# Edge stages of a two-layer graph network: when x is copied, how far gathers run ahead, when zeros are written, and in which order GpSimd waits

## What is computed

```python
h = maximum(layernorm(x), 0)                                   # layer 0
msgs = (h @ W0.T)[dst] * edge_weight[:, None]
x = x + segment_sum(msgs, src, N)
h = maximum(layernorm(x), 0)                                   # layer 1
h2 = segment_sum(h[src], dst, N) + h
h1 = h2 @ W1 + b1                                              # 256 -> 1024
h1 = relu((h1 - mean(h1, 0)) * rsqrt(var(h1, 0) + 1e-5) * gamma + beta)
out = x + relu(h1 @ W2 + b2)
```

## Time and profile before

| | |
|---|---|
| median of three runs | 4040.16 us |
| the profiled execution, whole | 4048.41 us |
| its span on the core | 4045.5 us |
| granted TensorE clock, mean of the span | 0.937 |
| layer 0, until its first scatter | 0 to 173.5 us |
| layer 0, scatters of groups 0 to 48 | 173.5 to 793 us |
| layer 1, until its first scatter | 793 to 843.3 us |
| layer 1, scatters of groups 0 to 48 | 843.3 to 1455 us |
| Gram, normalisation, main stage | 1455 to 4045 us |

### The profile page before, as it was taken

The page is one execution under the profiler, slowest core; times in us unless marked ns, Lnnn a source line. Parts: engine busy times, 40 slices in busy tenths (PEclk is TensorE's granted clock), DMA queues, the critical chain, the costliest instruction groups (busy, mean ns, idle before and its releaser), DMA issues.

```text
span 4045.5 us, 58701 instructions
## 1 busy us (share of the span) xinstructions
PE 3550.6 (88%) x17911; PEld 3028.4 (75%) x17911; DVE 2161.8 (53%) x5128; ACT 2164.8 (54%) x3631; POOL 1039.7 (26%) x801
## 2 busy tenths in 40 slices
PE   0387787488777869999999999999999999999999
PEld 0277777476666757778888888888888888888888
DVE  0355555366655568845555455455554555554554
ACT  0244454332222269956666656666666566566665
POOL 6377777678878720000000000000000000000000
PEclk9888878788888889999999999999999999999999
DMA  9966666567777789931211212212112122122120
GB/s 338 309 168 169 170 169 168 99 161 163 163 153 157 158 278 359 360 112 63 78 62 62 78 62 68 72 62 77 63 62 78 62 65 75 62 71 69 62 78 32
DMA packets 172586, 517.38 MB, mean 128 GB/s; under 512 B 26134, under 2 KB 78353, under 8 KB 166577
## 3 DMA queue, kind: packets, MB, share of 16 engines
q1 hardware_dynamic: 96160, 412.93, 30.0%
q0 software_dynamic: 75264, 102.81, 14.4%
q10 hardware_dynamic: 1072, 0.76, 0.1%
HBM read 361.58 MB, written 206.03 MB: 140 GB/s over the span
## 4 chain that ended last, share of the span: by engine, by line
PE 58%; POOL 16%; issue 10%; DMA 9%; ACT 5%; DVE 1%; ACTq 0%; POOLq 0%; another core or an unknown queue 0%; SPq 0%; DVEq 0%
PE ps_a L1204 27%; PE ps_b L1218 18%; PE ps_b L1219 9%; POOL agg_table L495 6%; POOL x_table L495 6%; DMA x_table<-in_x 4%; POOL arena L486 4%; DMA x_table<-arena,scatter_now 4%; ACT arena L621 4%; PE ps_a L1188 2%; DMA agg_table<-arena,scatter_now 1%; ACT arena_r L639 1%; PE ps_b L1115 0%; ACT arena L571 0%; PE ps_a L1167 0%
## 5 line engine op out<-in xcount | busy, mean ns | idle before, releaser
L1204 PE MATMUL ps_a<-arena_r 128*128 128x512 f32 (+1 forms) x4704 | 1197.2, 393 | 1.5 <-DVE arena_r L1027 1.5
L1218 PE MATMUL ps_b<-arena_r 128*128 128x512 f32 x3128 | 1138.5, 398 | 0.1
L1035 DVE TENSOR_TENSOR arena_r<-arena,arena_r 128x512 fp32r<-128x512 f32 (+1 forms) x784 | 539.9, 689 | 959.8 <-ACT arena_r L678 959.8
L673 ACT ACTIVATE arena<-ps_a,bn_bias,bn_scale 128x512 f32<-128x512 f32 (+1 forms) x784 | 607.7, 775 | 780.1 <-PE ps_a L1204 780.1
L1204 PEld LDWEIGHTS ps_a<-arena_r 128*128 128x128 f32 x4704 | 834.8, 188 | 178.7 <-ACT arena_r L664 1.9
L1219 PE MATMUL ps_b<-arena_r 128*128 128x256 f32 x3128 | 875.4, 280 | 0.0
L1218 PEld LDWEIGHTS ps_b<-arena_r 128*128 128x128 f32 x3128 | 587.2, 188 | 132.7 <-issue 0.4
L1219 PEld LDWEIGHTS ps_b<-arena_r 128*128 128x128 f32 x3128 | 589.6, 188 | 27.1
L678 ACT ACTIVATE arena_r<-arena 128x512 fp32r<-128x512 f32 (+1 forms) x784 | 494.8, 631 | 71.5
L1115 PE MATMUL ps_b<-arena,arena_r 128*128 128x256 f32 x1568 | 407.1, 425 | 0.0
L621 ACT ACTIVATE arena<-arena,norm_now 128x256 f32<-128x256 f32 (+1 forms) x782 | 403.5, 587 | 3.5 <-DVE norm_now L926 3.5
(11 more groups left out here) (116 smaller groups left out, 3904.5 us busy)
## 6 DMA issues: line engine op xcount, KB each, us to landing
arena<-x_table SPq DMA_DIRECT2D x291, 512.0 KB, 3.7
arena<-agg_table SPq DMA_DIRECT2D x194, 512.0 KB, 5.2
x_table<-in_x SPq DMA_DIRECT2D x10, 5000.0 KB
agg_table<-zeros SPq DMA_DIRECT2D x40, 1250.0 KB
out<-zeros SPq DMA_DIRECT2D x97, 512.0 KB, 6.0
arena<-in_x,gather_ids POOLq DMA_INDIRECT x196, 41.8
x_table<-arena,scatter_now POOLq DMA_INDIRECT x196
arena<-x_table,gather_ids POOLq DMA_INDIRECT x196
```

The source lines that it names most:

```text
L673: act.activation(hid[m % 2][:, 0:w], ps_a[:, 2 + m % 2, 0:w], ACT.Relu, scale=bn_scale[:, m:m + 1], bias=bn_bias[:, m:m + 1]).then_inc(hid ...
L1035: dve.tensor_tensor(hid_lo[m % 4][:, 0:w], hid[m % 2][:, 0:w], hid_hi[m % 4][:, 0:w].bitcast(F32), ALU.subtract).then_inc(hid_lo_ready, 1)
L1204: ins = pe.matmul(ps_a[:, 2 + m % 2, 0:w], w_part[:, kb, cols], h_part[:, kb, 0:w], start=(t == 0), stop=(t == len(terms) - 1))
L1218: pe.matmul(ps_b[0:p, r, :], hid_hi[m % 4][:, cols], w2, start=(m == 0), stop=(m == MB - 1), skip_group_check=True)
```

## The change

The copy of x is issued only when `dst` and all edge arrays that VectorE needs have landed. The ring of layer 0 has 16 slots instead of 20, and 15 groups instead of 22 are gathered before the first scatter; the other 34 groups are gathered between scatters. Zero piece i waits for group i of layer 0 to be retired, not for group i + 5 to be normalised. GpSimd waits for indices and message of group t + 1 before it waits for the landing of group t, and `pool_gate` is raised once in a layer there instead of at each group. The SBUF arena shrinks by four slots; an assertion is adapted.

```diff
-    RING = (20, 8)
-    LEAD = (22, 8)
+    RING = (16, 8)
+    LEAD = (15, 8)
...
+            sp.wait_ge(dst_loaded, LOAD_PARTS)
+            sp.wait_ge(info_loaded, 3 * LOAD_PARTS)
             copy_piece(0)
             copy_piece(1)
...
             def zero_piece(i):
-                sp.wait_ge(layers[0].normed_ready, i + AHEAD + 2)
+                sp.wait_ge(layers[0].retired, i + AHEAD + 1)
...
-            def scatter(l, t):
+            def wait_message(l, t):
                 pool.wait_ge(l.scatter_ready, t + 3)
                 pool.wait_ge(l.message_ready, t + 3)
-                pool.sem_inc(pool_gate, 1)
+
+            def scatter(l, t):
                 for a in range(QUAD):
...
+                wait_message(l, 0)
+                pool.sem_inc(pool_gate, 1)
                 for t in range(GROUPS):
                     scatter(l, t)
                     if t < GROUPS - 1:
                         for op in range(gathers_before(l, t), gathers_before(l, t + 1)):
                             gather(l, op)
+                        wait_message(l, t + 1)
                     pool.wait_ge(l.scattered[t % 2], (t // 2 + 1) * (16 * QUAD))
                     pool.sem_inc(l.retired, 1)
```

More of the change, by code:

```diff
@@ L145, in gnn_program @@
         rows_lo = [carve(arena_r, at, QUAD, D)[0] for at in (SLOT, 2 * SLOT)]
-        assert RING[1] <= 8 and RING[0] >= 19 and ROWS * D == SLOT
+        assert RING[1] <= 8 and RING[0] >= 16 and ROWS * D == SLOT
         agg_in = [carve(arena, s * SLOT, ROWS, D)[0] for s in range(LOADS)]
@@ L160, in gnn_program @@
         cov = [carve(arena, bn_at + k * D, D)[0] for k in range(KB)]
-        assert bn_at + KB * D <= RING[0] * SLOT
+        assert bn_at + KB * D <= SLOTS * SLOT
         w1_hi = carve(arena_r, 0, KB, HID)[0]
```

## The result

The changed kernel takes 3997.81 us (median of four runs, 3996.0 to 4003.1) against 4040.05 (four runs, 4038.31 to 4043.82): ratio 0.9896, 95% interval 0.9879 to 0.9914. The forecast was 3996.6 in a range of 3985 to 4021. The profiled execution took 3996.59 us, its span is 3994.4, 51.1 us less than the span before; some 13 of these 51 are chance of the first profile, as the first experiment shows.

The account below looks back on a forecast made before the run. It took the DMA backlog to bound the start, and scatter landings delayed by zeros or GpSimd's issue to bound layer 0. Terms -5.6, -37.6, -3.3, +3.9, -1.0 sum to -43.6: median 4040.2 to 3996.6 us, range 3985 to 4021.

Parts of the forecast that it names:

- start, until group 1: Before layer 0's group 1: the copy of x ends later, but fewer early gathers shorten the DMA backlog; -5.6 us.
- groups 1 to 39: Layer 0: zeros released by retired groups cut each of 39 periods from 12.545 to 11.58 us; -37.6 us.
- group 40: Layer 0: the vector loads behind its zero piece end 5.9 us earlier, so 11.6 instead of 14.87 us; -3.3 us.
- scatters 41 to 46: End of layer 0: later last gathers and longer groups make this stretch 62.5 instead of 58.6 us; +3.9 us.
- order of waits: Where a landing is last, about eight groups in layer 1 and three in layer 0, the gate's step goes; -1.0 us.
- boundary of the layers: Layer 1's first scatter waits 9.26 us after the gathers; no change forecast, bounds -9 (vanishes) to +10 (doubles).
- More gathers between scatters: Layer 0: 136 gathers in 45 groups instead of 108, three in each; costs nothing below a period of 11.58 us.
- TensorE: Layer 0: about 3 us idle a group exceeds the 0.97 taken away, so it does not become the next bound.
- half the gain of a group: Rival, layer 0: zero packets still push the last scatter past the third gather; period about 12.05 us, 4017 us; chance 0.12.
- no gain from moved zeros: Rival 2, layer 0: scatters need their DMA share wherever zeros lie; period 12.55 us, total 4036 us; chance 0.06.
- a lost start: Rival, start: no backlog left to shorten, the copy's later start is paid, +3 to +8 us; 4005 to 4010; chance 0.09.
- the slower one: Rival, layer 0: zeros delay the last scatter by 3.75 us; period 14.2 us, total 4104 us; chance 0.04.

Follow-up runs that it names:

- the first experiment: The kernel before, unchanged, timed and profiled once more (the repeated profile): median 4034.38 us, ratio 1.0002 to the kernel before beside it.
- the doubled zeros: The changed kernel with each zero piece written twice, the second to a table nobody reads: 4004.58 us, ratio 0.9923 to the kernel before.
- three times the zeros: The changed kernel with each zero piece written three times, two of them to tables nobody reads: 4116.07 us, ratio 1.0195 to the kernel before.

## Why the prediction was right, and where not

The sum was -43.6 us; the medians differ by 42.2. That they agree within 1.4 us is partly luck. Against the repeated profile the parts sum to -37.6 only, and the changed kernel with the old order of waits, the same within noise, came out 38.4 us below its neighbour. The mechanism held, and two terms, the start and the periods, were forecast 2.5 and 4 us too large. By parts, against the first profile of before and, in brackets, its repetition:

| part | forecast | measured |
|---|---|---|
| start, until group 1 | -5.6 | -7.1 (-3.1) |
| groups 1 to 39 | -37.6 | -34.1 (-33.5) |
| group 40 | -3.3 | -3.3 (-3.0) |
| scatters 41 to 46 | +3.9 | +3.8 (+3.7) |
| order of waits | -1.0 | 0 by two pairs of runs |
| boundary of the layers | 0 | -8.3 (-0.1) |
| layer 1, scatters 0 to 48 | in the -1.0 | -3.3 (0.0) |
| rest | 0 | +1.1 (-1.6) |

- **Zeros.** The step was right in mechanism and nearly in size: periods of 11.67 instead of 12.53, forecast 11.58. One term in it was mis-sized: the release. I put it at 10.7 us into the group, when the queue comes to its wait; `retired` is raised at 9.75, at the landing itself, which in four groups came 9.6 to 10.1 us into the group (forecast 9.5 to 10.5). The zeros are issued at 9.95, and their traffic begins under the third gather. The 0.09 us over 11.58 are in GpSimd's own time, since each first scatter follows after 0.30 us; I did not isolate what stretches it. The DMA sum of 8.8 us came out as 9.2 by the busy share, but the doubled zeros showed that such a sum does not say how much more fits in. The reading of the earlier trace rows was too simple: 427 GB/s holds until 408.70 only, then it is 290.
- **Start.** The sign was right, the size was not: -3.1 against the repeated profile, where -5.6 was forecast. The terms are opposite, as forecast. Copy later: +6.2 forecast for its end. It ended at 177.2, against 172.6 in the first profile and 168.6 in its repetition; the six profiles with the wait have it at 173.7 to 177.2, five with the copy at once, the first profile left out, at 168.3 to 169.7, 6.9 us apart in the mean. The mis-sized term is the gain from the index packets, 3 us less 1: from its first piece on the copy takes 166.8 us in the mean without them and 167.3 with them. At group 1 the wait costs 7.0 us by the kernel with the copy at once and 5.4 by 22 groups ahead with and without it (201.4 against 196.0). Fewer early gathers: -11 forecast, -9.5 and -8.5 measured. So the wait for the index loads is a loss, and it gives back more than half of what the shorter backlog brings.
- **More gathers between scatters.** "Costs nothing below 11.58" was right only because I compared with 12.55. The forecast took the change's parts together and never asked what two gathers a group would take once the zeros are out of the way: 10.68. Measured against that, the smaller ring costs the changed kernel 12 us by the spans, and 13 to 15 where the copy starts at once: the largest loss in it.
- **Tail.** 62.4 us against 62.5, by the chain from the last gather's start (707.15) to scatter 46 (722.13): 15.0 us, as in the earlier trace rows.
- **Order of waits.** The -1.0 was for places where a landing is last. Both comparisons show 0 within intervals of some 0.2% to each side; a microsecond can't be seen.
- **Boundary.** Rightly left at 0, but the wait of 9.26 us of the earlier trace rows was taken for a property of the kernel, with its bounds of -9 and +10. It was chance of one execution. That is one reason why the profiled executions differ by 51.8 us and the medians by 42.2.
- **TensorE.** Its idle time in the earlier trace rows rightly excluded it as the next bound: groups of 10.68 us ran without a wait for it, at a granted clock of 0.88 from 210 to 620 us, 0.81 before in the same stretch. The 3 us a group were read too high, since 39.6 of the 133.9 us are one wait ahead of group 1; without it they are 2.4.

The rivals: half the gain of a group, no gain from moved zeros and a lost start are excluded by the periods and by group 1's start in the changed kernel; the slower one needs three times the zeros. Of the signs of being wrong one could not decide anything: copy pieces over 34 us (35.11 and 36.94 here) stand in the kernel before as well (34.64 and 37.73). And a chance of 0.06 for rival 2, at 4036, does not fit with 0.04 for a change within 0.2%.

## What to carry to other kernels

When a chain of small dependent transfers shares the DMA with bulk writes that only have to be done some time, release the bulk by the event that opens the chain's next round, so that it is over before the round's last transfer is issued: one line brought 1.4% here. Then count again with the floor that is left: work that was hidden under the old wait is no longer free, and each part of a change should be tried without the others, since two of the four parts here, the copy's wait (7 us) and the smaller ring (12 us or more), gave back part of what the zeros had won. A wait without a releaser that is seen in one profile should be seen in a second before it is given a price.

## What was not expected of the hardware

- Copy, gathers and index loads share the DMA packet for packet, whatever the packets' size: 354, 355 and 345 packets from 60 to 120 us in the earlier trace rows, and 361 and 361 after. The copy's rate is the same with the index packets beside it and without (18.88 and 19.07 MB in 60 us; the gathers are there in both), so these small packets hardly slow it, while the gathers crawl (some 1 MB in 60 us).
- The DMA's busy share is no measure of the room that is left: at 0.79 another 1.28 MB a group fitted in with 0.18 us (0.97, 294 GB/s), and the next cost 2.75 us (0.99, 326 GB/s). The landing of the last scatter shows it better: 4.0, 5.0 and 7.8 us after its issue began, in the middle of the groups read.
- A gap of 9 us in VectorE and ScalarE at the boundary of the layers, in one profiled execution of the kernel before and in none of the thirteen other profiles; what caused it stays open.
